# A fused cross-attention and FP4 feed-forward kernel: the first group's queries and values in another order, the second group normalised earlier, the feed-forward weights loaded later

## The chip, the cores and the metric

The kernel runs on one core of one Trainium2 chip. The metric is the device time of one execution in microseconds (us), the median of the runs. The engines are PE (TensorE), DVE (VectorE), ACT (ScalarE), POOL (GpSimd) and SP (SyncE, which here only issues DMAs).

## The reference

64 sequences of 64 tokens with 128 features attend to contexts of 64 tokens with 256 features; then a feed-forward layer with block-wise FP4 quantisation follows, both with a residual.

```python
# x (64,64,128), ctx (64,64,256), mask (64,64)
n = layernorm(x)
kv = (ctx @ W_src.T + b_src) * mask       # keys and values, 8 heads of 16
q  = (n @ W_tgt.T + b_tgt) * mask
attn = softmax(where(mask == 0, -inf, q k^T / sqrt(16)))
x = x + concat(n, attn @ v) @ W_out.T + b_out
n = layernorm(x)
h = silu(fp4(n) @ fp4(w_gate).T) * (fp4(n) @ fp4(w_up).T)   # 352 wide
x = x + fp4(h) @ fp4(w_down).T
```

`fp4` scales blocks of 16 by their largest magnitude / 6 and rounds to eight magnitudes.

## The kernel before

The 4096 tokens are 8 groups (`NG`) of 512 (`GT`), each of 4 tiles of 128 tokens. A group passes through the attention as a pipeline: step `k` of a loop that every engine runs in its own written order (`attn_step(k)`) does the projections of group `k`, the scores and softmax of group `k-1`, the attention and the output projection of group `k-2`, and the statistics and quantisation for the feed-forward of group `k-3`. The feed-forward runs after the attention, 32 tiles one after the other. Everything is ordered by semaphores: each engine runs its list in order, and a `wait_ge` holds back all that stands behind it on that engine. Operands are float32.

PSUM has eight banks. The ones that matter here are `w0` (transposed `xn`, then queries, then values of the same group, each overwriting the last), `w1` (keys), `av_bank` (attention output; before that the target of warm-up multiplications), `o_bank` (output projection) and four banks of scores.

The start of the kernel, which the change touches, is this. SP issues the loads of tokens `x_all`, of contexts `cT`, of masks `mask_bc`, of the feed-forward weights `w_all` (`wg`, `wu`, `wd`), of `woT` and of `b_out`, in written order on one queue. The issue of the feed-forward weights waits for `w_zero`, which ACT sets after it has zeroed their padding.

DVE takes the statistics of group 0 (`stats1`), POOL computes the reciprocal deviation (`rstd1_only`, whose last instruction is the power at L264), and DVE normalises (`normalise1`, L717, four instructions of one tile). PE multiplies the keys of group 0 (`k_project`), transposes `xn` (L1104), runs 8 warm-up multiplications, and after DVE has copied `xnT` (L843) multiplies the queries (L1118). 10 more warm-ups follow while DVE adds the bias and multiplies the mask (`q_masked`, L731). Then come the scores of group 0 (L1051, L1061), its values (`v_project`, L1124, which wait for `qm_ok` since they overwrite the queries), the keys of group 1, the transposes of group 1, two `minus_max`, `bias_of_values` (L1041, which waits for `woT` and `b_out`), and the queries of group 1.

DVE in step 1 does: four row maxima (`row_max`, L739), `normalise1(1)`, the subtraction of a maximum (L748), the block maxima of the weights (L809, which wait for their loads), half of group 1's keys (L803), and `q_masked(1)` (L731). After `rstd1_only(1)`, POOL's next instruction is the conversion of the mask for groups 1 to 7 (L358). Between them it waits only for loads and for a memset that were issued in the first microseconds:

```python
rstd1_only(1)
pool.wait_ge(ld_mb, 16 * PAIRS)
pool.wait_ge(mb_zero, 2)
nc.gpsimd.tensor_scalar(neg_mask[:, TILES:, :], mask_b[:, TILES:, :], BIG, -BIG,
                        ALU.mult, ALU.add).then_inc(nm_ok, 1)
```

Of the kernel before, what the change touches and what calls it, by code (L numbers as in the profile page):

```python
# [7 lines left out]
ALU = mybir.AluOpType  # L8
# [3 lines left out]
P = 128  # L12
# [5 lines left out]
TILES = 4  # L18
GT = TILES * P
NG = B * S // GT  # L20
NT = NG * TILES
PAIRS = H // 2
# [22 lines left out]
def on(g):  # L45
    return 0 <= g < NG
# [13 lines left out]
def xattn_ffn(nc, x, ctxT, mask_pairs, mask_rows, WsT, bkvq, WtT, WoT, bo, wg, wu, wd, out):  # L60
    with ExitStack() as ctx:
# [3 lines left out]
        def sem(name):  # L65
            return ctx.enter_context(nc.semaphore(name))


        ident = sb("ident", [P, P])
# [110 lines left out]
        pad_ok = sem("pad_ok")  # L180
        sub_ok = sem("sub_ok")
        calm_ok = sem("calm_ok")
        up_tile_ok, round_tile_ok = sem("up_tile_ok"), sem("round_tile_ok")
        w_thirds = (slice(0, WBLK // 2), slice(WBLK // 2, WBLK), slice(WBLK, WALL))

# [3 lines left out]
        def past(eng, semaphore, value):  # L189

            if value > 0:
                eng.wait_ge(semaphore, value)
# [8 lines left out]
        def _(sp):  # L201
# [26 lines left out]
            load_x(1)  # L228
            load_c(1)
            sp.wait_ge(w_zero, 2)  # L230
            for r, w in ((0, wg), (1, wu)):
                sp.dma_start(w_all[0:WP, r * WBLK // 2:(r + 1) * WBLK // 2, :].rearrange("p (r n) k -> p r (n k)", r=WR),
                             w.rearrange("(r p) k -> p r k", p=WP)).then_inc(ld_fw, 16)
# [255 lines left out]
        def _(act):  # L489
# [10 lines left out]
            def v_evac(g):  # L500
                s = g % 2
                act.wait_ge(pe_v, g + 1)
                past(act, pe_av, g - 1)
                act.wait_ge(v_zero, 2)
                vp = w0[:, :].rearrange("r (t p e d) -> r t p e d", t=TILES, p=PAIRS, e=2)
                for b in range(2):
                    for e in range(2):
                        last = nc.scalar.copy(val[s][64 * e:64 * e + 64, :, b, :, HD * e:HD * (e + 1)],  # L508
                                              vp[64 * b:64 * b + 64, :, :, e, :])
                last.then_inc(v_ok, 1)  # L510
# [181 lines left out]
        def _(dve):  # L692
# [32 lines left out]
            def q_masked(g):  # L725
                dve.wait_ge(pe_q, g + 1)
                dve.wait_ge(ld_m[g], 16)
                if g == 0:
                    dve.wait_ge(ld_b, 16)
                past(dve, pe_s, g - 1)  # L730
                nc.vector.scalar_tensor_tensor(out=q_m[g % 2][:, :], in0=w0[:, :], scalar=b_q,  # L731
                                               in1=mask_bc[:, g * GT:(g + 1) * GT],
                                               op0=ALU.add, op1=ALU.mult).then_inc(qm_ok, 1)
# [105 lines left out]
            dve.wait_ge(ld_b, 16)  # L839
            nc.vector.tensor_scalar(bk_of[:, :], head_of[:, :], b_k, None, ALU.mult).then_inc(c_bk, 1)  # L840
            normalise1(0)
            dve.wait_ge(pe_xnT, 1)
            nc.vector.tensor_copy(xnT[0][:, :], w0[:, :]).then_inc(xnT_ok, 1)  # L843

            def attn_step(k):
                g1, g2, g3, g4 = k, k - 1, k - 2, k - 3
# [3 lines left out]
                if on(g2):  # L850
                    for p in range(PAIRS):
                        row_max(g2, p)
                if k == 1:
                    normalise1(1)
                if on(g3):
                    update(g3)
                if on(g2) and k < NG:
# [5 lines left out]
                    k_block(1, 1)  # L863
                if k == 2:
                    weights_round_up(0)
                if on(g1):
                    q_masked(g1)
                if k < 2:
                    stats1(k + 1)
# [167 lines left out]
        def _(pe):  # L1037
# [6 lines left out]
            def scores(g):  # L1044
# [4 lines left out]
                for p in range(PAIRS):  # L1049
                    r = slice(32 * p, 32 * p + 2)  # L1050
                    nc.tensor.matmul(s_bank[p][:, :], sel[r, :, :].rearrange("r b s -> r (b s)"),  # L1051
                                     neg_mask[r, tiles(g), :].unsqueeze(2).to_broadcast([2, TILES, 2, S]),
                                     start=True, stop=False, skip_group_check=True)
                pe.wait_ge(qm_ok, g + 1)
                pe.wait_ge(k_ok, 2 * g + 2)
                for j in range(TILES):
# [42 lines left out]

            def xn_transpose(g):  # L1100
                pe.wait_ge(xn_ok, g + 1)
                past(pe, v_ok, g)
                for j in range(TILES):
                    last = nc.tensor.transpose(w0[:, j * P:(j + 1) * P], xn[g % 2][:, j, :], ident[:, :])  # L1104
                last.then_inc(pe_xnT, 1)

            def k_project(g):
                pe.wait_ge(ld_ws, 16)
# [9 lines left out]
                nc.tensor.matmul(w0[:, :], wtT[:, :], xnT[g % 3][:, :], start=True, stop=True).then_inc(pe_q, 1)  # L1118

            def v_project(g, half):  # L1120
                pe.wait_ge(qm_ok, g + 1)
                for j in (2 * half, 2 * half + 1):
                    for c in range(2):
                        last = nc.tensor.matmul(w0[:, j * P:(j + 1) * P], cT[g % 4][:, c, j * P:(j + 1) * P],  # L1124
                                                wsT[:, c, D:2 * D], start=(c == 0), stop=(c == 1))
                if half:
                    last.then_inc(pe_v, 1)
# [99 lines left out]
            def attn_step(k):  # L1227
# [1 line left out]
                if on(g2):  # L1229
                    scores(g2)  # L1230
                if k == 1:
                    v_project(0, 0)
                    v_project(0, 1)
                    k_project(1)
                if on(g3):
# [1 line left out]
                    spread_reciprocals(g3)  # L1237
                if k == 0:
                    k_project(0)
                    xn_transpose(0)  # L1240
                    warm_up(8)
                    q_project(0)
                    warm_up(10)
                elif on(g1):
                    xn_transpose(g1)
                    if k > 1:
                        k_project(g1)
# [80 lines left out]
```

## Time and profile before

| | |
|---|---|
| median of 3 runs | 195.92 us (195.89 to 197.83) |
| the profiled execution | 195.77 us |
| its span, first to last instruction | 193.6 us |
| mean granted TensorE clock | 0.999 |
| busy share of PE, DVE, ACT, POOL | 95%, 92%, 68%, 72% |

The span leaves 2.17 us of the profiled execution outside it. Busy shares are means over the whole execution; times in the rows further down count from the start of the span.

### The profile page before, as it was taken

The numbers are of one execution on the slowest core, as the hardware profiler recorded it, in microseconds if no ns is written. First come the engines' busy times: TensorE is split into PE (matmuls) and PEld (weight loads), VectorE is DVE, ScalarE is ACT, GpSimd is POOL, SyncE is SP. The second block draws the span as 40 slices with busy tenths as digits, with TensorE's granted clock in tenths as the row PEclk, the third lists the DMA queues.
The fourth block names the chain that finished last, engine by engine and source line by source line (L and its number), as shares of the span: only waits on it lengthen the run. The fifth ranks groups of instructions, "written<-read, shape, count | busy, mean of one in ns | idle before, by whom it ended". The sixth has DMA issues, their size and how long they took to land.

```text
span 193.6 us, 5839 instructions
## 1 busy us (share of the span) xinstructions
PE 183.7 (95%) x2098; PEld 141.9 (73%) x2098; DVE 178.9 (92%) x402; ACT 130.8 (68%) x277; POOL 138.9 (72%) x205
## 2 busy tenths in 40 slices
PE   7899989999999999999999999899899999899985
PEld 7574857859768588597786767567777786677884
DVE  6689999899999999999978999999999999999992
ACT  3507889869779688796877844475566673666761
POOL 6333595576698997984928489697999985777770
PEclk9999999999999999999999999999999999999999
DMA  5799339450210000000000000000101010101005
GB/s 190 249 258 322 144 97 302 147 168 3 65 48 3 0 3 3 2 0 5 3 0 3 3 2 0 0 5 2 54 0 54 3 54 0 54 5 56 0 3 163
DMA packets 13698, 11.99 MB, mean 62 GB/s; under 512 B 790, under 2 KB 10590, under 8 KB 13670
## 3 DMA queue, kind: packets, MB, share of 16 engines
q1 hardware_dynamic: 13086, 11.23, 18.8%
q10 hardware_dynamic: 584, 0.39, 0.6%
q8 instruction: 17, 0.28, 0.6%
q14 instruction: 11, 0.09, 0.1%
HBM read 9.52 MB, written 2.10 MB: 60 GB/s over the span
## 4 chain that ended last, share of the span: by engine, by line
POOL 35%; PE 27%; issue 17%; DVE 14%; DMA 2%; ACT 2%; POOLq 1%; ACTq 0%; DVEq 0%
POOL wq_y L404 10%; POOL hq L419 8%; PE bank L1124 5%; POOL sch L411 3%; POOL xn L291 3%; PE bank L1112 3%; DVE mx L739 3%; DMA wsT<-in_WsT 2%; PE a_pair L1075 2%; DVE st L700 2%; POOL rs L281 2%; DVE den L757 2%; PE bank L1087 2%; PE bank L1061 2%; PE bank L1075 2%
## 5 line engine op out<-in xcount | busy, mean ns | idle before, releaser
L1215 PE MATMUL bank<-wdT,hT 128*128 128x128 f32 x186 | 26.2, 277 | 1.7 <-issue 1.6
L1180 PE MATMUL bank<-guT,xqT 128*128 128x352 f32 x64 | 24.7, 468 | 1.0 <-DVE hh L910 0.9
L1215 PEld LDWEIGHTS bank<-wdT,hT 128*128 128x128 f32 x186 | 23.2, 191 | 2.6 <-issue 2.3
L1183 PE MATMUL bank<-guT,xqT 128*128 128x352 f32 x64 | 24.2, 459 | 0.0
L404 POOL TENSOR_TENSOR wq_y<-hh,ivh 128x704 f32<-128x704 f32 x15 | 21.2, 1411 | 3.0 <-ACT ivh L651 2.4
L419 POOL TENSOR_TENSOR hq<-wq_u,sch 128x704 f32<-128x704 f32 x14 | 19.4, 1389 | 4.6 <-DVE wq_u L936 4.4
L757 DVE TENSOR_REDUCE den<-prob 128x8 f32<-128x512 f32 x32 | 19.8, 665 | 0.0
L645 ACT COPY hT<-bank 128x384 f32<-128x384 f32 x32 | 15.2, 474 | 4.1 <-PE bank L1195 4.1
L1124 PE MATMUL bank<-wsT,cT 128*128 128x128 f32 x128 | 17.4, 280 | 0.5 <-DVE q_m L731 0.4
L632 ACT ACTIVATE a_pair<-wq_y 128x704 f32<-128x704 f32 x15 | 11.5, 765 | 8.8 <-DVE wq_u L936 7.4
L1183 PEld LDWEIGHTS bank<-guT,xqT 128*128 128x128 f32 x64 | 12.1, 190 | 6.8 <-ACT mask_bc L566 0.2
L526 ACT ACTIVATE k_bd<-bank,bk_of,head_of 128x512 f32<-128x512 f32 x15 | 11.6, 780 | 7.8 <-PE bank L1112 7.8
L1124 PEld LDWEIGHTS bank<-wsT,cT 128*128 128x128 f32 x128 | 15.4, 191 | 1.8 <-DVE q_m L731 1.6
L1195 PEld LDWEIGHTS bank<-ident,hq 128*128 128x128 f32 x96 | 12.0, 141 | 6.5 <-issue 3.1
L566 ACT ACTIVATE mask_bc<-bank 128x352 f32<-128x352 f32 x32 | 14.7, 459 | 2.9 <-PE bank L1180 2.6
L1195 PE MATMUL bank<-ident,hq 128*128 128x128 f32 x96 | 15.8, 274 | 0.8 <-POOL hq L442 0.6
L910 DVE TENSOR_TENSOR hh<-bank,mask_bc 128x352 f32<-128x352 f32 x32 | 15.9, 498 | 0.3 <-ACT mask_bc L566 0.3
L1112 PE MATMUL bank<-cT,wsT 128*128 128x512 f32 x32 | 15.1, 595 | 0.5 <-DMA wsT<-in_WsT 0.5
L508 ACT COPY val<-bank 64x256 f32<-64x256 f32 x32 | 11.7, 365 | 5.3 <-PE bank L1124 5.0
L918 DVE TENSOR_REDUCE amh<-hh 128x44 f32<-128x748 f32 x16 | 14.9, 929 | 0.4
L291 POOL TENSOR_SCALAR xn<-x_all,nm,rs 128x128 f32<-128x128 f32 x32 | 14.0, 452 | 0.8
L700 DVE BATCH_NORM_STATS2 st<-x_all 128x6 f32<-128x128 f32 x64 | 13.6, 275 | 0.9 <-DMA x_all<-in_x 0.7
(144 smaller groups left out, 507.5 us busy)
## 6 DMA issues: line engine op xcount, KB each, us to landing
cT<-in_ctxT SPq DMA_DIRECT2D x8, 512.0 KB, 5.6
x_all<-in_x SPq DMA_DIRECT2D x8, 256.0 KB, 6.0
mask_bc<-in_mask_rows SPq DMA_DIRECT2D x8, 256.0 KB, 6.2
out_y<-mask_bc SPq DMA_DIRECT2D x7, 256.0 KB, 2.2
wsT<-in_WsT ACTq DMA_DIRECT2D x1, 256.0 KB, 4.8
out_y<-x_all SPq DMA_DIRECT2D x1, 192.0 KB, 2.0
w_all<-in_wg SPq DMA_DIRECT2D x1, 176.0 KB
w_all<-in_wu SPq DMA_DIRECT2D x1, 176.0 KB
```

The costliest lines, as they stand in the source:

```text
L291: last = nc.gpsimd.tensor_scalar(xn2[:, j * NB_X:(j + 1) * NB_X, :].rearrange("p n k -> p (n k)"), x_all[:, n, :], nm2[:, n:n + 1], rs2[:, ...
L404: nc.gpsimd.tensor_tensor(yh[i][:, :, :], hh[i][:, :, 0:BLK], ivh[i][:, :].unsqueeze(2).to_broadcast([P, 2 * NB_H, BLK]), ALU.mult).then_i ...
L419: nc.gpsimd.tensor_tensor(hq[i][:, :, 0:I].rearrange("p t (n k) -> p t n k", k=BLK), rh[i][:, :, :].rearrange("p (t n) k -> p t n k", t=2) ...
L700: last = nc.vector.bn_stats(st[:, n, :], x_all[:, n, :])
L757: nc.vector.tensor_reduce(den[:, :, p, :], prob[g % 2][p][:, :, :].rearrange("r j (e s) -> r j e s", e=2), AX.X, ALU.add).then_inc(sum_ok, 1)
L910: nc.vector.tensor_tensor(hh[u % 2][:, t * NB_H:(t + 1) * NB_H, 0:BLK], gu_bank[(2 * n + 1) % 3][:, 0:I].rearrange("p (n k) -> p n k", k=BLK),
L1112: last = nc.tensor.matmul(w1[:, :], wsT[:, c, 0:D], cT[g % 4][:, c, :], start=(c == 0), stop=(c == 1))
L1124: last = nc.tensor.matmul(w0[:, j * P:(j + 1) * P], cT[g % 4][:, c, j * P:(j + 1) * P], wsT[:, c, D:2 * D], start=(c == 0), stop=(c == 1))
L1180: nc.tensor.matmul(gu_bank[2 * n % 3][:, 0:I], xqT[g % 2][:, t], guT[:, 0, :], start=True, stop=True).then_inc(pe_g, 1)
L1183: nc.tensor.matmul(gu_bank[(2 * n + 1) % 3][:, 0:I], xqT[g % 2][:, t], guT[:, 1, :], start=True, stop=True).then_inc(pe_u, 1)
L1195: last = nc.tensor.transpose(t_bank[place % 2][:, c * P:(c + 1) * P], hq[u % 2][:, n % 2, c * P:(c + 1) * P], ident[:, :])
L1215: last = nc.tensor.matmul(bank[:, j * P:(j + 1) * P], hT[n % 2][:, c, :], wdT[:, c, :], start=(c == 0), stop=(c == 2))
```

## The change

Four things are changed. First, the transposed tokens and the queries of group 0 are handled in halves of two tiles: the first half in `w0`, the second in `o_bank`, and DVE copies and masks half by half. Second, the values of group 0 go to `av_bank`, so that their first half (tiles 0 and 1) is multiplied between the transposes and the queries, in the place of the warm-ups, and only their second half stays behind the scores. The transposes of group 1 no longer wait for the copy of group 0's values. Third, DVE normalises group 1 after the second of the four row maxima and not after the fourth. Fourth, SP issues the feed-forward weights, and with them everything behind them on its queue, only after group 0's transposes (`pe_xnT`).

```diff
--- before.py
+++ after.py
@@ -180,6 +180,8 @@
         pad_ok = sem("pad_ok")
         sub_ok = sem("sub_ok")
         calm_ok = sem("calm_ok")
+        pe_xh, xh_ok, pe_qh, qh_ok = sem("pe_xh"), sem("xh_ok"), sem("pe_qh"), sem("qh_ok")
+        halves, half_bank = (slice(0, GT // 2), slice(GT // 2, GT)), (w0, o_bank)
         up_tile_ok, round_tile_ok = sem("up_tile_ok"), sem("round_tile_ok")
         w_thirds = (slice(0, WBLK // 2), slice(WBLK // 2, WBLK), slice(WBLK, WALL))
 
@@ -228,6 +230,7 @@
             load_x(1)
             load_c(1)
             sp.wait_ge(w_zero, 2)
+            sp.wait_ge(pe_xnT, 1)
             for r, w in ((0, wg), (1, wu)):
                 sp.dma_start(w_all[0:WP, r * WBLK // 2:(r + 1) * WBLK // 2, :].rearrange("p (r n) k -> p r (n k)", r=WR),
                              w.rearrange("(r p) k -> p r k", p=WP)).then_inc(ld_fw, 16)
@@ -502,7 +505,7 @@
                 act.wait_ge(pe_v, g + 1)
                 past(act, pe_av, g - 1)
                 act.wait_ge(v_zero, 2)
-                vp = w0[:, :].rearrange("r (t p e d) -> r t p e d", t=TILES, p=PAIRS, e=2)
+                vp = (w0 if g > 0 else av_bank)[:, :].rearrange("r (t p e d) -> r t p e d", t=TILES, p=PAIRS, e=2)
                 for b in range(2):
                     for e in range(2):
                         last = nc.scalar.copy(val[s][64 * e:64 * e + 64, :, b, :, HD * e:HD * (e + 1)],
@@ -725,8 +728,6 @@
             def q_masked(g):
                 dve.wait_ge(pe_q, g + 1)
                 dve.wait_ge(ld_m[g], 16)
-                if g == 0:
-                    dve.wait_ge(ld_b, 16)
                 past(dve, pe_s, g - 1)
                 nc.vector.scalar_tensor_tensor(out=q_m[g % 2][:, :], in0=w0[:, :], scalar=b_q,
                                                in1=mask_bc[:, g * GT:(g + 1) * GT],
@@ -839,8 +840,16 @@
             dve.wait_ge(ld_b, 16)
             nc.vector.tensor_scalar(bk_of[:, :], head_of[:, :], b_k, None, ALU.mult).then_inc(c_bk, 1)
             normalise1(0)
-            dve.wait_ge(pe_xnT, 1)
-            nc.vector.tensor_copy(xnT[0][:, :], w0[:, :]).then_inc(xnT_ok, 1)
+            for h in range(2):
+                dve.wait_ge(pe_xnT if h else pe_xh, 1)
+                nc.vector.tensor_copy(xnT[0][:, halves[h]], half_bank[h][:, 0:GT // 2]).then_inc(xnT_ok if h else xh_ok, 1)
+            dve.wait_ge(ld_m[0], 16)
+            dve.wait_ge(ld_b, 16)
+            for h in range(2):
+                dve.wait_ge(pe_q if h else pe_qh, 1)
+                nc.vector.scalar_tensor_tensor(out=q_m[0][:, halves[h]], in0=half_bank[h][:, 0:GT // 2], scalar=b_q,
+                                               in1=mask_bc[:, halves[h]],
+                                               op0=ALU.add, op1=ALU.mult).then_inc(qm_ok if h else qh_ok, 1)
 
             def attn_step(k):
                 g1, g2, g3, g4 = k, k - 1, k - 2, k - 3
@@ -850,8 +859,8 @@
                 if on(g2):
                     for p in range(PAIRS):
                         row_max(g2, p)
-                if k == 1:
-                    normalise1(1)
+                        if k == 1 and p == 1:
+                            normalise1(1)
                 if on(g3):
                     update(g3)
                 if on(g2) and k < NG:
@@ -863,7 +872,7 @@
                     k_block(1, 1)
                 if k == 2:
                     weights_round_up(0)
-                if on(g1):
+                if on(g1) and k > 0:
                     q_masked(g1)
                 if k < 2:
                     stats1(k + 1)
@@ -1051,6 +1060,8 @@
                     nc.tensor.matmul(s_bank[p][:, :], sel[r, :, :].rearrange("r b s -> r (b s)"),
                                      neg_mask[r, tiles(g), :].unsqueeze(2).to_broadcast([2, TILES, 2, S]),
                                      start=True, stop=False, skip_group_check=True)
+                if g == 0:
+                    pe.wait_ge(qh_ok, 1)
                 pe.wait_ge(qm_ok, g + 1)
                 pe.wait_ge(k_ok, 2 * g + 2)
                 for j in range(TILES):
@@ -1099,10 +1110,22 @@
 
             def xn_transpose(g):
                 pe.wait_ge(xn_ok, g + 1)
-                past(pe, v_ok, g)
+                past(pe, v_ok, g if g > 1 else 0)
                 for j in range(TILES):
                     last = nc.tensor.transpose(w0[:, j * P:(j + 1) * P], xn[g % 2][:, j, :], ident[:, :])
                 last.then_inc(pe_xnT, 1)
+
+            def first_transpose(h):
+                pe.wait_ge(xn_ok, 1)
+                for j in range(2):
+                    last = nc.tensor.transpose(half_bank[h][:, j * P:(j + 1) * P], xn[0][:, 2 * h + j, :], ident[:, :])
+                last.then_inc(pe_xnT if h else pe_xh, 1)
+
+            def first_queries(h):
+                pe.wait_ge(ld_wt, 16)
+                pe.wait_ge(xnT_ok if h else xh_ok, 1)
+                nc.tensor.matmul(half_bank[h][:, 0:GT // 2], wtT[:, :], xnT[0][:, halves[h]],
+                                 start=True, stop=True).then_inc(pe_q if h else pe_qh, 1)
 
             def k_project(g):
                 pe.wait_ge(ld_ws, 16)
@@ -1118,10 +1141,12 @@
                 nc.tensor.matmul(w0[:, :], wtT[:, :], xnT[g % 3][:, :], start=True, stop=True).then_inc(pe_q, 1)
 
             def v_project(g, half):
-                pe.wait_ge(qm_ok, g + 1)
+                bank = w0 if g > 0 else av_bank
+                if g > 0:
+                    pe.wait_ge(qm_ok, g + 1)
                 for j in (2 * half, 2 * half + 1):
                     for c in range(2):
-                        last = nc.tensor.matmul(w0[:, j * P:(j + 1) * P], cT[g % 4][:, c, j * P:(j + 1) * P],
+                        last = nc.tensor.matmul(bank[:, j * P:(j + 1) * P], cT[g % 4][:, c, j * P:(j + 1) * P],
                                                 wsT[:, c, D:2 * D], start=(c == 0), stop=(c == 1))
                 if half:
                     last.then_inc(pe_v, 1)
@@ -1229,7 +1254,6 @@
                 if on(g2):
                     scores(g2)
                 if k == 1:
-                    v_project(0, 0)
                     v_project(0, 1)
                     k_project(1)
                 if on(g3):
@@ -1237,10 +1261,11 @@
                     spread_reciprocals(g3)
                 if k == 0:
                     k_project(0)
-                    xn_transpose(0)
-                    warm_up(8)
-                    q_project(0)
-                    warm_up(10)
+                    first_transpose(0)
+                    first_transpose(1)
+                    v_project(0, 0)
+                    first_queries(0)
+                    first_queries(1)
                 elif on(g1):
                     xn_transpose(g1)
                     if k > 1:
```

## Rows read from the trace of the kernel before

**Rows 1.** The page: busy time by engine, DMA in 40 slices of 4.84 us

```profile
PE 183.7 (95%) x2098; PEld 141.9 (73%) x2098; DVE 178.9 (92%) x402; ACT 130.8 (68%) x277; POOL 138.9 (72%) x205
...
DMA  5799339450210000000000000000101010101005
```

**Rows 2.** The chain in order of time, 0 to 60 us: start us, us, what

```profile
8.04 0.45 PE bank L1104 x4
...
23.05 1.78 POOL wq_y L376
...
41.85 0.86 PE bank L1118 x2
...
43.92 0.89 PE bank L1124 x8
```

**Rows 3.** The timeline of PE, 8 to 19 us: start us, us, engine, what

```profile
9.35 1.10 PE L1118 MATMUL bank<-xnT,wtT 128*128 128x512 f32 x2 [0.43 <-DVE xnT L843]
...
17.43 0.38 PE L1041 MATMUL bank<-woT,b_kvq 128*128 128x128 f32 x2
17.93 1.10 PE L1118 MATMUL bank<-xnT,wtT 128*128 128x512 f32 x2
```

**Rows 4.** The timeline of DVE, 8 to 20 us: start us, us, engine, what

```profile
8.52 0.69 DVE L843 COPY xnT<-bank 128x512 f32<-128x512 f32 x1 [0.94 <-PE bank L1104]
10.49 0.75 DVE L731 SCALAR_TENSOR_TENSOR q_m<-bank,b_kvq,mask_bc 128x512 f32<-128x512 f32 x1 [1.28 <-PE bank L1118]
...
12.05 0.38 DVE L705 BATCH_NORM_AGGREGATE mv<-st 128x2 f32<-128x6 f32 x4
12.54 1.29 DVE L739 TENSOR_REDUCE mx<-bank 128x8 bf16<-128x512 f32 x2
...
14.94 1.52 DVE L717 TENSOR_SCALAR xn<-x_all,mv,rs 128x128 f32<-128x128 f32 x4
16.38 0.68 DVE L748 TENSOR_TENSOR prob<-a_pair,mx 128x512 f32<-128x512 f32 x1
16.98 1.60 DVE L809 TENSOR_REDUCE wq_am<-w_all 128x88 f32<-128x1408 f32 x1
18.58 0.81 DVE L803 TENSOR_SCALAR k_bd<-bank,head_of,bk_of 128x512 f32<-128x512 f32 x1
19.30 0.74 DVE L731 SCALAR_TENSOR_TENSOR q_m<-bank,b_kvq,mask_bc 128x512 f32<-128x512 f32 x1
```

**Rows 5.** The timeline of POOL, 12 to 17 us

```profile
12.80 1.01 POOL L264 TENSOR_TENSOR rs<-ve,minus_half 128x4 f32<-128x4 f32 x1
13.89 1.69 POOL L358 TENSOR_SCALAR neg_mask<-mask_b 128x1792 bf16<-128x1792 f32 x1
```

**Rows 6.** The line of normalise1 (L717): one instruction each of group 0 and group 1

```profile
6.46 0.35 DVE L717 TENSOR_SCALAR xn<-x_all,mv,rs 128x128 f32<-128x128 f32 x1 [0.22 <-POOL rs L264]
...
14.94 0.73 DVE L717 TENSOR_SCALAR xn<-x_all,mv,rs 128x128 f32<-128x128 f32 x1
```

**Rows 7.** The timelines of DVE and POOL at 47 and 86 us

```profile
47.52 0.66 DVE L829 SCALAR_TENSOR_TENSOR wq_u<-wq_a,wq_u 128x512 f32<-128x512 f32 x1
48.10 0.69 DVE L792 SCALAR_TENSOR_TENSOR u<-a,y 128x512 f32<-128x512 f32 x1
...
47.70 0.55 POOL L268 TENSOR_SCALAR ve<-mv 128x4 f32<-128x4 f32 x1 [0.55 <-DVE mv L705]
...
86.62 1.21 DVE L796 SCALAR_TENSOR_TENSOR r<-a,u 128x512 f32<-128x512 f32 x1
...
86.06 1.22 POOL L305 TENSOR_TENSOR w_all<-wq_u,wq_nsc 128x384 f32<-128x384 f32 x1 [0.49 <-DVE wq_u L829]
```

**Rows 8.** SP's issues, and the landing of b_out: KB, us from issue to landing

```profile
5.99 0.33 SPq L232 DMA_DIRECT2D w_all<-in_wg  x1
...
11.79 1.01 SPq L238 DMA_DIRECT2D b_out<-in_bo  x1
...
b_out<-in_bo SPq DMA_DIRECT2D x1, 64.0 KB, 5.2
```

## The prediction

> **What bounds the kernel now.** I read the page first. PE and DVE are both above nine tenths busy [rows 1], so a change that starts the pipeline sooner or later moves the end by as much, unless an engine waits there anyway. The change touches only the first 20 us, so the question is who sets the pace there. In the chain in order of time, PE and DVE alternate until the queries of group 0 are masked; from there the chain runs over DVE, then over POOL's product of the weights and on to PE [rows 2]. I then read DVE's own timeline [rows 4]. Before the masked queries (10.49) DVE waited 1.28 us for PE. From 10.49 on no row of DVE has an idle time: row maxima, normalisation, subtraction, weight maxima, keys and masked queries of group 1 stand end to end until 20.04. PE and ACT wait for DVE in this stretch. So the sum asks two things: when DVE can begin its unbroken run, and how long that run is. I measure at the end of the masked queries of group 1, 20.04 us; what follows depends on it on all engines, and I let its shift pass to the end undiminished.
>
> **Part 1, halves and values in front.** PE finishes the keys at 8.04 and needs 0.45 us for four transposes [rows 2], so the first half is there at 8.26 and the second at 8.49. The whole copy takes 0.69 us and the masking 0.75 [rows 4] for 512 columns. A half of 256 columns has no row; it lies between half the time and the whole of it. An instruction on 128 columns took 0.35 [rows 6]; on a straight line from there to the whole, a half copy takes 0.46 and a half masking 0.48. Two copies end at about 9.2. They don't decide: PE has the eight instructions of half the values between (0.89 for eight [rows 2]), 8.49 to 9.38, so the copy is hidden. Two half queries at 0.43 each (0.86 for the whole [rows 2]) end at 9.85 and 10.28. In the kernel before the queries ended at 10.45 [rows 3]. Masking the first half runs while PE multiplies the second, so only a half is left behind it: 10.28 plus 0.48 is 10.76, against 11.24 before (10.49 plus 0.75). Gain 0.48 us; from 0.2 (a half as dear as the whole, 10.28 + 0.75) to 0.6 (half the price, 10.28 + 0.38). The rest of the values, one half and not two, stays behind the scores; PE becomes free 0.9 us sooner but must then wait for DVE's normalisation, so this is worth nothing more by itself. The second value half in `av_bank`, the dropped wait for `v_ok` and the moved waits for loads cost nothing, as PE waited for DVE there and the mask had landed before 10.49.
>
> **Part 2, the warm-ups dropped.** The first eight give way to real work. The gap between the queries and the scores was filled by warm-ups; now it is about 0.5 us with four short multiplications in it. I take zero; the other end is a rival below. The Trainium skill's page "TensorE: Matmul & The Clock Gate", section "What's actually happening", says that a clock gate passes only half of the clock's pulses when PE has been little busy. The trace of before shows the full clock all through, so it can't show what a lost warm-up does; by this rule the time would be that of rival D.
>
> **Part 3, group 1 normalised after two maxima.** This is the step that decides. By order alone it costs DVE nothing: the same instructions, other order. But see what happens on POOL at that time. The power for group 1 ends at 13.81 and the mask conversion begins at 13.89 and runs until 15.58 [rows 5]. In the kernel before DVE spent 13.74 to 15.02 on row maxima, that is beside it. When it then came to normalise at 14.94, the first instruction took 0.73 us where that of group 0, with POOL idle, took 0.35 [rows 6], and the four together ended 0.88 after POOL's conversion (16.46 against 15.58). So DVE's normalisation doesn't run beside POOL's conversion: 0.38 us were lost even there. Two further places say how such a conflict is decided. At 47.70 POOL's instruction came during a DVE instruction and ended 0.07 after it (48.25 against 48.18), though the next of DVE had already begun at 48.10. At 86.06 POOL came during a DVE instruction, got its turn behind it, and the next of DVE took 1.21 us [rows 7] where its like takes 0.69. POOL thus gets in between two instructions of DVE, and the later one waits for all of POOL's.
>
> In the new order all times behind the masked queries of group 0 are 0.48 sooner. DVE's statistics, then POOL's power follow: the power ends at 13.33. The first two maxima start at 12.06 (12.54 less 0.48) and end at 13.35. So DVE's normalisation and POOL's conversion become ready within 0.1 us of each other, both released by the same power. If POOL is first, it holds 13.41 to 15.10; if DVE is first, it gets one instruction of 0.35 done and POOL's 1.69 us stand in front of the other three. Either way the normalisation ends 0.88 behind a conversion that ends at 15.10, or somewhat later with less to do behind it: 15.98. Two maxima are then still to come, two steps of 0.60 (12.54 to 13.74 for two [rows 4]), where before the subtraction could begin at once at 16.38. Now it begins at 15.90 + 1.20 = 17.10. That is 0.72 later than before: 0.48 gained, 1.2 us of maxima no longer beside POOL's conversion. With the weights there, the rest of the run follows: weight maxima, keys, masked queries at 20.04 + 0.72 = 20.76.
>
> The Trainium skill's page "SBUF — State Buffer", section "Who interferes with whom", says that such a DVE instruction and a GpSimd one need the same pair of ports, and that the one that issues second blocks fully. If it were only the first that holds all four back to back, and DVE came first, the time would be that of rival B; the rows at 47 and 86 us speak for turns by the instruction.
>
> **Part 4, the loads.** SP issued the first weights at 5.99 [rows 8]; now it waits for the transposes' end at 8.49, so they and all behind them are issued up to 2.6 us later. How much of that arrives? The DMA engines' work stays the same, so only the time is lost in which they now stand idle for want of transfers. The slice from 4.8 to 9.7 us was seven tenths busy, those from 9.7 to 19.4 nine or more [rows 1]; token group 1 and context 1, issued before, are still under way. The loss lies between 0 (they fill the wait) and 2.6 (nothing does), and I take 0.8, nearer to zero, because the slice in question had three tenths of it idle already. The tightest user is `bias_of_values` on PE: `b_out` was issued at 11.79 and landed 5.2 later at 17.0 [rows 8], and PE used it at 17.43 [rows 3]. Behind that wait on PE stand the queries of group 1 (they ended at 19.03 [rows 3]), a subtraction and the transposes of the probabilities; DVE's masking waits for the queries. With 0.8 the bias is multiplied at 17.85 and the queries end at about 19.1, before DVE gets to them at 20.02. The cover is 0.9 us; if it goes, the price is what exceeds it. The weights' own landing has no row: no one waited for them at 16.98 [rows 4], and now they are needed at 17.70. Context 1, which lies in front of them, can only come sooner.
>
> **The sum.** -0.48 (part 1) + 1.20 (part 3) + 0 (parts 2 and 4) = +0.72 us on 195.77, or 196.5. The profiled execution lies 0.15 below the median of the runs, so on their scale it is 196.6. Bounds from the terms: part 1 between 0.2 and 0.6, part 3 between 1.2 and 1.7: 196.4 to 197.3.
>
> **Rivals.** (A) The forecast, port conflict, 196.6: chance 0.57.
> (B) The conflict doesn't occur as in rows 6: DVE's four instructions run through, 1.12 us, and POOL's conversion waits, needed only by the scores of group 1, which come after their queries. Then the gain of 0.48 stays and the 0.38 lost before is won back, 0.86 in all, but now DVE reaches the queries of group 1 at 18.44, and PE ends them at 18.2 (if `b_out` comes as before) to 19.1 (0.8 later). The gain is 0.86 or 0.2: 195.1 to 195.7, middle 195.3. Against it stand the rows at 47 and 86 us, for it that these are other instructions. Chance 0.25.
> (C) The loads decide, slower than before: if the whole 2.6 us reach `b_out`, it lands at 19.6, the queries end at 20.85 and DVE masks until 21.6, +1.55: 197.5. It decides from a shift of 1.7 us on. For it: the DMA engines are full; against it: the loads issued ahead fill part of the hole. Chance 0.10.
> (D) The clock falls to 1.2 GHz without the warm-ups, and 3.4 us of PE work between 8.04 and 12.5 double: 199.2. PE has no long pause there. Chance 0.03.
> (E) The end is set by something else and nothing moves: 195.9. Chance 0.05.
>
> **How the numbers follow.** A single run of this kernel can't tell less than about 1%, 2 us, from nothing. A, B, E and nearly all of C lie within it: 0.90. Faster by over 1% has 0.03 (it would need more than all of part 1 and part 3 can give), slower by over 1% has 0.07: D, and a C above its price or on top of A. The range holds A and B with their bounds and stops short of C's end: 194.9 to 197.4.
>
> **What would show it.** In the profile after: masked queries of group 0 ending at about 10.8; the second half's copy before the values end; the normalisation of group 1 starting at 13.4 with one instruction stretched by 1.3 us or more, and the last two maxima behind it at 16; POOL's conversion at 13.4; weight maxima and queries of group 1 without an idle time of DVE in front of them, ending at 20.8. Four short instructions of L717 there would show B; an idle time of DVE ahead of L731 released by PE, and PE idle ahead of L1041, would show C; a granted clock below 1, D. The prediction is wrong above all if instructions of DVE that follow each other closely keep POOL out.

## The result

| | before | changed |
|---|---|---|
| median of 20 runs each | 195.75 us | 197.4 us |
| ratio, changed to before | | 1.0076, 95% interval 1.0055 to 1.0097 |
| span of the profiled execution | 193.6 us | 195.5 us |

The change makes the kernel slower by 0.76%, 1.5 us (1.1 to 1.9). 196.6 us was forecast, with a range of 194.9 to 197.4: the sign and the chain of causes at the start were right, the size was half of what was measured, and the median lies on the range's upper edge.

The first fence is DVE's timeline of the changed kernel, and answers to [rows 4]; columns as there.

```profile
8.55 0.75 DVE L845 COPY xnT<-bank 128x256 f32<-128x256 f32 x2 [0.98 <-PE bank L1121]
10.21 0.88 DVE L850 SCALAR_TENSOR_TENSOR q_m<-bank,b_kvq,mask_bc 128x256 f32<-128x256 f32 x2 [0.91 <-PE bank L1127]
...
11.90 0.38 DVE L708 BATCH_NORM_AGGREGATE mv<-st 128x2 f32<-128x6 f32 x4
12.43 1.29 DVE L740 TENSOR_REDUCE mx<-bank 128x8 bf16<-128x512 f32 x2
13.70 2.60 DVE L720 TENSOR_SCALAR xn<-x_all,mv,rs 128x128 f32<-128x128 f32 x4
16.22 1.27 DVE L740 TENSOR_REDUCE mx<-a_pair 128x8 bf16<-128x512 f32 x2
17.53 0.69 DVE L749 TENSOR_TENSOR prob<-a_pair,mx 128x512 f32<-128x512 f32 x1
18.14 1.61 DVE L810 TENSOR_REDUCE wq_am<-w_all 128x88 f32<-128x1408 f32 x1
19.66 0.80 DVE L804 TENSOR_SCALAR k_bd<-bank,head_of,bk_of 128x512 f32<-128x512 f32 x1
20.38 0.74 DVE L732 SCALAR_TENSOR_TENSOR q_m<-bank,b_kvq,mask_bc 128x512 f32<-128x512 f32 x1
```

Four things are to be read. The two half copies and half maskings are there, and masking starts at 10.21 and not at 10.49. The normalisation (now L720) has moved ahead of the last two maxima, starts at 13.70 and takes 2.60 us, where it took 1.52. There is no idle time in front of any row after it. The masked queries of group 1 start at 20.38, 1.08 later than before (19.30 in [rows 4]). The next fences show POOL beside it (as [rows 5]) and the first of DVE's four normalising instructions alone (as [rows 6]).

```profile
12.65 1.01 POOL L267 TENSOR_TENSOR rs<-ve,minus_half 128x4 f32<-128x4 f32 x1
13.74 1.69 POOL L361 TENSOR_SCALAR neg_mask<-mask_b 128x1792 bf16<-128x1792 f32 x1
```

```profile
13.70 1.82 DVE L720 TENSOR_SCALAR xn<-x_all,mv,rs 128x128 f32<-128x128 f32 x1
```

POOL's conversion of the mask, released like DVE by the power at L267, is recorded 0.04 us behind the start of DVE's first instruction. Yet that instruction takes 1.82 us, where its like took 0.35 with POOL idle, and it ends 0.09 us after the conversion.

The loads, on SP's timeline and in the list of landings (as [rows 8]), and the bias on PE's timeline (as [rows 3]):

```profile
8.83 0.33 SPq L235 DMA_DIRECT2D w_all<-in_wg  x1
...
11.62 1.10 SPq L241 DMA_DIRECT2D b_out<-in_bo  x1
...
b_out<-in_bo SPq DMA_DIRECT2D x1, 64.0 KB, 5.3
...
17.28 0.38 PE L1050 MATMUL bank<-woT,b_kvq 128*128 128x128 f32 x2
```

The first weights were issued 2.8 us later than before, but `b_out` was issued 0.17 us earlier, since SP's issues no longer stalled, and landed at 16.92. PE used it at 17.28 without waiting.

This explains 1.08 us. Comparing the start of the same instructions of DVE through both traces, the difference shrinks slowly to 1.03 us at 89 us, grows by 0.17 there, and is 1.14 us at the last instruction of DVE (192.39 and 191.25). The spans differ by 1.9. So 0.76 us more are lost behind the last computation, where only the stores are left. The fences show what the DMA engines moved from 189.8 us to the end, in 40 slices of 0.155 us, and the last store's time to landing; first the kernel before, then the changed one.

```profile
GB/s 340 327 350 337 106 63 297 353 344 347 291 27 0 76 334 337 360 331 245 10 0 0 0 0 0 0 0 0 0 0 0 0 0 53 0 0 0 0 0 0
...
out_y<-x_all SPq DMA_DIRECT2D x1, 64.0 KB, 1.6
```

```profile
GB/s 0 0 0 0 0 106 79 317 317 330 330 314 324 324 330 334 189 13 13 23 20 155 344 357 337 337 182 26 20 23 20 17 0 0 0 0 0 0 0 0
...
out_y<-x_all SPq DMA_DIRECT2D x1, 64.0 KB, 2.3
```

Before, the last stores' data flows at about 330 to 360 GB/s and stops. In the changed kernel each of the two bursts ends in a tail at 13 to 26 GB/s, near a sixteenth of the full rate, as if one of the 16 DMA engines were behind the rest. The last store lands in 2.3 us and not in 1.6. What else was on the queues is in the same view of one microsecond each, 188 to 189 us for the kernel before and 190 to 191 for the changed one: the last large block of instructions. The columns are the number of packets, MB, and the time that they took as a share of the 16 engines. A share of 7.8% of 16 engines in one microsecond is 1.25 us of one engine, 9.7% is 1.55. In the kernel before the block starts at 188.5 and is over when the stores' data begins at 189.7; in the changed one it starts at 190.6, 0.2 us ahead of their first data, and takes up one engine until 192.1. Queue q8 moves 17 such blocks in the whole execution, which fits PE alone: it has 2098 multiplications and as many weight loads, no other engine more than 402 instructions that count as busy.

Before:

```profile
q8 instruction: 1, 0.02, 7.8%
```

Changed:

```profile
q8 instruction: 1, 0.02, 9.7%
```

### The profile page after: what moved, and what is told of

It is laid out like the page before. It is cut to its first block, busy times and chain, and to the rows that moved or that the text cites. A ratio compares the mean times of both kernels' runs of the same rounds, so it can differ in the third digit from the quotient of the medians.

```text
span 195.5 us, 5810 instructions
## 1 busy us (share of the span) xinstructions
PE 182.7 (93%) x2082; PEld 141.3 (72%) x2082; DVE 180.2 (92%) x404; ACT 130.7 (67%) x277; POOL 138.5 (71%) x205
## 4 chain that ended last, share of the span: by engine, by line
POOL 35%; PE 26%; issue 18%; DVE 14%; DMA 2%; ACT 2%; POOLq 1%; ACTq 0%; DVEq 0%
POOL wq_y L407 10%; POOL hq L422 8%; PE bank L1149 5%; POOL sch L414 3%; POOL xn L294 3%; DVE mx L740 3%; PE bank L1135 3%; DMA wsT<-in_WsT 2%; PE a_pair L1086 2%; DVE st L703 2%; POOL rs L284 2%; PE bank L1098 2%; DVE den L758 2%; PE bank L1072 2%; PE bank L1086 2%
## 5 line engine op out<-in xcount | busy, mean ns | idle before, releaser
L635 ACT ACTIVATE a_pair<-wq_y 128x704 f32<-128x704 f32 x15 | 11.5, 765 | 8.7 <-DVE wq_u L945 7.3
```

## The experiments

Each ratio is to the kernel before on the same chip. "Queries" is the start of the masked queries of group 1 on DVE, "rest" the time from the end of DVE's last instruction to the end of the span, "store" the last 64 KB store, issue to landing, all from the profiled execution.

| kernel | queries | rest | store | ratio (interval) |
|---|---|---|---|---|
| before | 19.30 | 2.1 | 1.6 | 1 |
| changed | 20.38 | 2.8 | 2.3 | 1.0076 (1.0055 to 1.0097) |
| early normalisation alone | 20.48 | 2.1 | 1.6 | 1.0064 (1.0051 to 1.0076) |
| late loads alone | 19.53 | 2.1 | 1.6 | 0.9991 (0.9968 to 1.0013) |
| halves alone | 18.93 | 3.0 | 2.5 | 1.0037 (1.0008 to 1.0066) |
| changed, normalisation late | 18.82 | 2.6 | 2.1 | 1.0027 (1.0008 to 1.0046) |
| changed, POOL waits | 18.56 | 2.7 | 2.2 | 1.0010 (0.9974 to 1.0045) |
| changed, conversion twice | 21.81 | 2.9 | 2.4 | 1.0153 (1.0115 to 1.0192) |
| changed, conversion first | 19.86 | 2.7 | 2.2 | 1.0071 (1.0042 to 1.0100) |
| changed, PE's list refilled | 20.08 | 2.1 | 1.6 | 1.0032 (1.0008 to 1.0055) |
| POOL waits, list refilled | 19.16 | 2.1 | 1.6 | 0.9977 (0.9952 to 1.0002) |
| the same, loads early | 19.20 | 2.1 | 1.6 | 0.9976 (0.9952 to 1.0000) |
| before, POOL waits | 19.06 | 2.1 | 1.6 | 0.9980 (0.9955 to 1.0005) |
| before, conversion first | 21.08 | 2.1 | 1.6 | 0.9996 (0.9965 to 1.0027) |

### The parts one by one

**Normalisation back behind four maxima**, everything else as changed:

```diff
-                        if k == 1 and p == 1:
-                            normalise1(1)
+                if k == 1:
+                    normalise1(1)
```

> The changed kernel, with the normalisation of group 1 back behind all four row maxima. Port theory (POOL's mask conversion holds up DVE's normalisation): the first instruction of the normalisation falls from 1.82 to about 0.7 us, as before the change, and the masked queries of group 1 start 0.1 to 0.3 us sooner than in the kernel before (19.0 to 19.2, against 20.38 in the changed one); the time is 0.1 to 0.3 us below the kernel before, where the changed one is 1.5 above. Load theory (the late weights and what stands behind them cost the time): the time stays 1.0 us or more above the kernel before.

The queries came at 18.82, 1.56 sooner than in the changed kernel, and the ratio fell from 1.0076 to 1.0027. The load theory falls. But DVE's chain was 0.48 us ahead of the kernel before and the time was not below it as expected. In the profiled execution the gain was spent at the end, with the slow last store: 0.41 us were left at DVE's last instruction, the rest was 0.5 longer, and its time of 195.76 us is level with the kernel before. The 0.27% on top come from executions that were not profiled (four of the twelve took 196.3 to 197.5 us), and their cause is open.

**The same move alone**, in the kernel before:

```diff
                     for p in range(PAIRS):
                         row_max(g2, p)
-                if k == 1:
-                    normalise1(1)
+                        if k == 1 and p == 1:
+                            normalise1(1)
```

> The kernel before, with nothing changed but the place of group 1's normalisation, behind two row maxima. Port theory: one instruction of 1.8 us, the masked queries of group 1 start 1.2 us later than before, the time is 1.2 us (1.0 to 1.5) above the kernel before. Load theory: no difference (within 0.3 us).

Measured, in five runs: one instruction of 1.82 us, queries 1.18 later, 1.0064 (1.25 us). The store is as quick as before. This one move carries most of the loss.

The stretched instruction there, on DVE's timeline:

```profile
13.79 1.82 DVE L717 TENSOR_SCALAR xn<-x_all,mv,rs 128x128 f32<-128x128 f32 x1
```

**The late loads alone:**

```diff
             sp.wait_ge(w_zero, 2)
+            sp.wait_ge(pe_xnT, 1)
```

> The kernel before, with nothing changed but the wait of SP for group 0's transposes ahead of the feed-forward weights. Port theory: no difference (within 0.2 us), b_out lands at 16.9 to 17.8 and DVE has no idle time ahead of the masked queries of group 1. Load theory: 0.4 to 1.5 us above the kernel before.

0.9991, interval on both sides of 1: no difference. The queries start 0.23 later, but so do those of group 0 (10.72), before any of the moved loads is used. PE began the keys of group 0 at 6.32 in this execution and not at 6.09. `b_out` landed at 18.1, later than expected, and PE waited 0.28 us for it; DVE had no idle time ahead of the queries.

**The halves and the values in front alone** (no early normalisation, no late loads):

```diff
-                        if k == 1 and p == 1:
-                            normalise1(1)
+                if k == 1:
+                    normalise1(1)
-            sp.wait_ge(pe_xnT, 1)
```

> The kernel before with the halves and the values in front alone (normalisation behind four row maxima, weights loaded at once). DVE's masked queries of group 1 start 0.2 to 0.5 us sooner; the gain is spent at the end, where PE's shorter list puts the loading of its last piece on the last stores (64 KB store 2.1 to 2.3 us): the time lies within 0.3 us of the kernel before, more likely above. If the late weights had a part in the slow stores, the store takes 1.6 us here.

The queries came 0.37 sooner, and 0.27 of it was left at DVE's last instruction; the time is 0.37% above. So this part is a gain where it was meant to be one, and a loss as a whole. The loads aren't late here, and the store took 2.5 us: the late loads have no part in that.

### The port

**POOL's conversion held back:**

```diff
+            pool.wait_ge(xn_ok, 2)
             pool.wait_ge(ld_mb, 16 * PAIRS)
             pool.wait_ge(mb_zero, 2)
```

> The changed kernel, with POOL's mask conversion for groups 1 to 7 held back until group 1 is normalised. Port theory: the four instructions take 1.1 us together, the first 0.35, and the masked queries of group 1 start at about 18.8; the time is 0.4 to 0.6 us below the kernel before. Load theory: still 1.0 us or more above it. Order theory (the two late row maxima cost by themselves): between the two, near or above the kernel before.

DVE's timeline and POOL's:

```profile
13.37 1.12 DVE L721 TENSOR_SCALAR xn<-x_all,mv,rs 128x128 f32<-128x128 f32 x4
14.40 1.28 DVE L741 TENSOR_REDUCE mx<-a_pair 128x8 bf16<-128x512 f32 x2
```

```profile
14.57 1.69 POOL L362 TENSOR_SCALAR neg_mask<-mask_b 128x1792 bf16<-128x1792 f32 x1 [1.24 <-DVE xn L721]
```

The four instructions took 1.12 us, with the two late maxima behind them and POOL's conversion beside those, and the queries came at 18.56, 1.82 us sooner than in the changed kernel. From the end of group 0's masking to group 1's DVE needed 7.80 us, against 7.69 in the next run, where the maxima stand in their old order: the order costs 0.1 us at most, POOL's conversion the rest. The time missed its expectation: it is level with the kernel before. Of 0.74 us of lead at 19 us, 0.48 were left at 89 us (0.24 of it went between 80 and 86 us, for a cause that is open), 0.35 at DVE's last instruction, and the rest of the span was 0.6 longer.

**The same wait in the kernel before:** 

> The kernel before, with only POOL's mask conversion held back until group 1 is normalised. Port theory: the first normalising instruction of group 1 falls from 0.73 to 0.35 us, the masked queries start 0.38 us sooner, and the time is 0.3 to 0.4 us below the kernel before. If the port has no part in it: no difference.

The normalisation took 1.11 us (0.34 for the first instruction), and from group 0's queries to group 1's DVE needed 0.37 us less. The ratio of 0.9980 fits the 0.35 us by which its last instruction came sooner, though its interval still holds 1.

**The conversion twice:**

```diff
+            nc.gpsimd.tensor_scalar(spare[:, :, :], mask_b[:, TILES:, :], BIG, -BIG, ALU.mult, ALU.add)
             nc.gpsimd.tensor_scalar(neg_mask[:, TILES:, :], mask_b[:, TILES:, :], BIG, -BIG,
```

> The changed kernel, with POOL's conversion of the mask done twice in a row, first into a spare tile. Port theory, turns by the instruction: DVE's first normalising instruction gets in behind the first conversion or behind both; if behind the first, the second conversion goes in front of the next one of DVE, so the four together take about 4.3 us (2.60 + 1.69) either way, and the time is about 3.0 us above the kernel before. Theory that the first requester keeps the port for its run, and DVE gets it after one conversion for all four: the four stay at 2.6 us and the time at 1.5 above.

DVE's four instructions took 4.10 us, and the time was 1.53% above the kernel before, the 3.0 us expected. Its timeline in short stretches shows the first two singly:

```profile
13.63 1.82 DVE L722 TENSOR_SCALAR xn<-x_all,mv,rs 128x128 f32<-128x128 f32 x1
...
15.36 1.83 DVE L722 TENSOR_SCALAR xn<-x_all,mv,rs 128x128 f32<-128x128 f32 x1
```

Each of the first two waited for one conversion (POOL's began at 13.68 and 15.43). So the two engines take turns by the instruction, as the rows at 47 and 86 us had it, and a run of DVE instructions is no cover against a POOL instruction that is waiting. This kernel also shows the lower level of PE's clock (0.50 of the full one, 1.2 GHz). PE, waiting for DVE most of the time, was busy for 0.21 of the 2 us from 16 to 18; from 20 to 22 us the granted clock was 0.50, and the queries of group 1 took 2.04 us where they took 1.10 in the changed kernel. They were done at 21.25, still before DVE came to mask them at 21.81.

**The conversion ahead of group 1's statistics**, in POOL's idle time:

```diff
-            rstd1_only(1)
             pool.wait_ge(ld_mb, 16 * PAIRS)
 ...
+            rstd1_only(1)
```

> The changed kernel, with POOL's conversion moved ahead of its work for group 1's statistics, into its idle time. Port theory: the conversion runs when the mask pairs have landed, between 8 and 12 us, the four normalising instructions take 1.1 us, and the masked queries of group 1 start at 18.6 as with POOL waiting; DVE's chain is 0.7 us ahead of the kernel before, the end 0.2 less because of the slower last store. If the mask pairs land after 11 us the power is late and the gain is lost.

The second case came true. POOL's timeline:

```profile
11.56 1.69 POOL L360 TENSOR_SCALAR neg_mask<-mask_b 128x1792 bf16<-128x1792 f32 x1 [4.05 <-DMA mask_b<-in_mask_pairs]
...
13.62 1.01 POOL L267 TENSOR_TENSOR rs<-ve,minus_half 128x4 f32<-128x4 f32 x1
```

The mask pairs landed only at 11.5, the power ended 1.3 us late, DVE waited 1.18 us for it, and the gain was gone. Its four instructions took 1.12 us, as expected without the conversion beside them.

**The same in the kernel before:** 

> The kernel before, with only POOL's conversion moved ahead of its work for group 1's statistics. Port theory: the first normalising instruction of group 1 falls from 0.73 to 0.35 us, DVE's chain gains 0.38 us and the time falls by 0.3 to 0.4 us. If the port has no part in it: no difference.

Ratio 0.9996 (0.9965 to 1.0027), which tells nothing. The four instructions took 1.11 us. In its profiled execution the keys of group 0 took 3.75 us where they else take 2.0, and everything behind was late, so its start times can't be compared with the others. The distance can: from group 0's queries to group 1's DVE needed 8.44 us, as with POOL waiting, and 8.81 in the kernel before.

### The end

**PE's list filled up again:**

```diff
+            def refill(count):
+                pe.wait_ge(k_ok, 2)
+                for _ in range(count):
+                    nc.tensor.matmul(w1[:, 0:P], calm[:, :], calm[:, :], start=True, stop=True)
...
                     v_project(0, 1)
+                    refill(8)
                     k_project(1)
...
                     first_queries(1)
+                    refill(10)
```

> The changed kernel, with 18 warm-up multiplications put back into PE's list (10 behind the halves of the queries, 8 ahead of group 1's keys, both into the keys' bank), so that its length is near that of before. Code-loading theory (PE's instruction list is 32 instructions shorter, so that the loading of its last piece falls on the last stores): the time from DVE's last instruction to the end of the span falls from 2.8 to 2.1 us, the 64 KB store from 2.3 to 1.6, and the later row maxima at 90 us lose no 0.17 us; the time is about 1.1 us above the kernel before, or a little more for the warm-ups ahead of the scores. Rival (the stores are slow by chance or because of the late loads): the 64 KB store stays at 2.1 to 2.3 us.

Eighteen multiplications whose result nobody reads bring the ratio from 1.0076 to 1.0032. Of these 0.9 us, 0.75 lie behind DVE's last instruction (a rest of 2.07 for 2.82) and the remainder at the front, where the keys of group 0 began 0.08 and ended 0.3 sooner. The DMA engines' view of 189.8 us to the end and the last store:

```profile
GB/s 0 106 0 0 3 261 330 327 344 304 53 23 20 89 314 357 344 353 248 155 340 357 347 334 172 0 0 0 0 0 0 0 0 0 0 0 0 0 0 53
...
out_y<-x_all SPq DMA_DIRECT2D x1, 64.0 KB, 1.6
```

Behind the last burst the tail is gone, and the last store takes 1.6 us again; a short tail (53 23 20) is left behind the first burst. The step of 0.17 us near 90 us is still there (0.75 before it, 0.93 behind it), so that isn't caused by PE's list. The last block of code, from the view of 189 to 190 us:

```profile
q8 instruction: 1, 0.02, 5.9%
```

It starts at 190.0 here and takes 0.94 us of one engine. The stores' data begins at 190.6, so the two overlap by 0.3 us, where it was 1.3 in the changed kernel.

**POOL waits and the list filled up**, the candidate for a better kernel: the wait of above, `warm_up(52)` for 42 at PE's start, and `refill(7)` behind the halves of the queries.

> The changed kernel with POOL's mask conversion held back until group 1 is normalised, and 17 warm-ups put back into PE's list, 10 at its start where PE waits for the keys' weights and 7 behind the halves of the queries. Masked queries of group 1 start at 18.6, the last store takes 1.6 us, 2.1 us from DVE's last instruction to the end; the chain gives back 0.3 to 0.4 us near 90 us as in the run with POOL waiting. Time 0.3 to 0.6 us below the kernel before.

> The same with the feed-forward weights loaded at once, as in the kernel before. If the order of the loads is worth nothing, within 0.2 us of the other one; b_out then still lands at about 17.0, and PE waits for it up to 1 us, without DVE noticing.

0.9977 and 0.9976, 0.45 us below the kernel before, at the edge of what 12 runs can tell. The store took 1.6 us in both, and the order of the loads is worth nothing. But the queries came at 19.16 and 19.20, not 18.6: the ten more warm-ups at the start ran past the landing of the weights of the keys, so that PE began the keys at 6.49 and not at 6.1. PE also waited for `b_out` there, until 17.8 in the first of the two, which DVE didn't notice beyond 0.1 us. Neither is clearly better than the kernel before with its one added wait (0.9980).

## Why the prediction came out as it did

**Which engine sets the pace.** Right. DVE has no idle time from group 0's queries to group 1's in any of the kernels but those where POOL or PE's warm-ups held it up. A shift there passed on to 89 us within 0.1 us in nine of the thirteen; in the other four (the three changed kernels in which POOL waits, and the kernel before with the conversion first) it changed by 0.2 to 0.3 us on the way, in one against the kernel and in three in its favour, so "undiminished" holds only to within 0.3 us.

**Part 3, the normalisation.** Right in place, cause and size. 1.2 us was the term; the move alone cost 1.18 at the queries and 1.25 us of time. The stretched instruction, its place and its cause are as told. One detail was not borne out: if DVE came first it was to get one instruction done. It was recorded as first by 0.04 us and waited nevertheless, which made no difference to the sum. The Trainium skill's page "SBUF — State Buffer", section "Who interferes with whom", says that the later one is blocked for the whole instruction of the other; the trace agrees (1.82 us beside a conversion of 1.69). What the run with two conversions adds is that a run of four doesn't hold the port between them, so rival B, the one that this rule read over the whole run would give, is out.

**Part 1, the halves.** Right in the mechanism, 0.48 forecast, 0.37 and 0.48 measured in two kernels (halves alone, normalisation late). In the profiled execution of the change itself only 0.15 of the forecast 0.48 was left, mostly because the keys of group 0 took 2.17 us there and 1.96 before. That belongs to the execution and not to the change (last section).

**Part 2, the warm-ups dropped.** This is the step that failed: "I take zero". In the changed kernel the clock was at its full level from 6.6 us until PE had finished, so rival D is out. (The prediction read the kernel before as at the full clock all through; its trace has the first entry of the clock at 5.4 us, and nothing ahead of it.) But the instructions had a second effect that the prediction doesn't have at all: PE's list became 16 multiplications and 16 weight loads shorter (2082 for 2098), and with that the loading of its last block fell on the last stores. Measured: 0.5 to 1.0 us more between the last instruction and the end in all six kernels with the short list, and none in the three where the list was filled up. That the loading block is what holds one DMA engine back is an inference from the tail's rate, a sixteenth, from the 1.55 us that the block takes of one engine, and from its time; that filling up PE's list takes the loss away is shown, with the multiplications put in at different places (10 and 8, or 10 and 7). The Trainium skill's page "Runtime: NRT & Kernel Launch", section "Instruction fetch mechanics", says that instructions are loaded in blocks of 16 KiB over a DMA queue, and that the engine's slow pace hides it. The first agrees with the 0.02 MB of the row; the second speaks of the engine, and the loss here lies in the stores that use the DMA engines at the same time.

**Part 4, the loads.** Zero was right. `b_out` was to land 0.8 us later, at 17.8; it landed at 16.9 in the changed kernel and at 18.1 with the late loads alone, and PE used it at 17.77 and 17.57 in the last two kernels, one with late loads and one without. So its landing varies by more than the change moves it. At 18.1 PE waited 0.28 us, and the queries of group 1 ended at 19.45, 0.08 us before DVE came to mask them: the cover that the prediction named was nearly used up there, and DVE still had no idle time. SP's issue of `woT` took 0.51 us where it took 2.41 before, so the queue caught up. Rival C needed 1.7 us and didn't come.

**The sum.** 0.72 forecast at the queries, 1.08 measured in that execution; the halves' 0.33 less is the difference. The shift was 1.14 at DVE's last instruction, the 0.17 near 90 us included, and with the 0.76 at the end the spans differ by 1.9, the medians by 1.65. The forecast's own terms had allowed 196.4 to 197.3. That 197.4 still lies in the range is luck: 0.76 us of the loss come from the end of the kernel, and about 0.2 each from the step near 90 us and from the late keys of this execution, and the prediction has none of the three. What makes the 0.17 is open: all kernels with the halves have it, filled up or not, and none of those without the halves does. It arises between the aggregation of a group's statistics and its first row maximum, whose starts lie 0.44 us apart there and 0.30 in the kernel before. DVE's own list grew by two instructions and some waits; no run tells whether that is it.

## What to carry to other kernels

When two engines are released by the same instruction, look at what each does next: a move on one of them by a microsecond can put it on the other's longest instruction, and holding the unimportant one back by a wait can give the loss back (here 0.35 us in the kernel before). And the last stores share the DMA engines with the loading of code, as far as these traces tell: a change in the length of an engine's list, even by instructions that do nothing, can move a block onto them, so the stretch behind the last computation belongs in every comparison of two traces. A column that says full clock ahead of the trace's first entry of the clock shows nothing; the time of one multiplication does.

## What was not expected

The last store took 1.6 us in all kernels with PE's list near its old length, and 2.1 to 2.5 us in the others. DVE's instruction that is recorded first by 0.04 us still waited for POOL; the records don't tell which of the two came first.

And the keys of group 0, the same four instructions in all kernels, took between 1.94 and 2.17 us, once 3.75. The profile's column of the granted clock says 1.00 in that stretch of all of them, but the multiplications themselves say otherwise. The rows are the keys of group 0 in the changed kernel, the same in the kernel before with the conversion first, and the queries of group 1 in the run with two conversions (ns min/median/max), with the stretch of 20 to 22 us of the latter, where the column says 0.50:

```profile
L1135 PE MATMUL bank<-cT,wsT x4: 593/593/887, 6.1 to 7.7; 128*128 128x512 f32 x4
...
L1112 PE MATMUL bank<-cT,wsT x4: 1061/1061/1192, 6.2 to 8.9; 128*128 128x512 f32 x4
...
L1143 PE MATMUL bank<-xnT,wtT x2: 1061/1126/1192, 19.2 to 20.2; 128*128 128x512 f32 x2
...
20.00:22.00 2.00, 2.00 (x6) 0.91 (x5) 2.00 (x3) 1.00 (x3) 0.00 (x0) 0.50 0.69 266
```

The slow keys ran at the pace of the lower level, 1061 ns where it is 593 at the full one. Each trace has a first entry of the clock, at the full level; ahead of it there is none, and the column then says 1.00. In ten of the fourteen kernels this entry comes before the keys begin, and they take 1.94 to 1.96 us. In the other four it comes behind their start: at 6.4, 6.6 and 6.9 us, with keys of 2.10 to 2.17 us, and at 10.3 us, with keys of 3.75. So the clock rose late in those executions. The two kernels with ten more warm-ups at the start have it at 6.5 and 6.9 us, so these didn't bring it forward. That accounts for 0.2 us of the changed kernel's start, and may be what makes single executions of every kernel about 2 us longer (two of the twenty of the kernel before); no trace of those shows it.
